# One block for the whole program, with one stage semaphore in place of the block ends of a graph network kernel

## The chip, the cores and the metric

The kernel runs on one core of one Trainium2 chip. The metric is the device time of one execution in microseconds (us); lower is better. The median of three executions is 4856.15 us.

## The reference

The input is a graph of 6250 nodes with 256 features and 100000 edges, sorted by destination. A layer norm and a ReLU are followed by three rounds of message passing with a maximum; the result is added to `x`; a second layer norm and ReLU are followed by one layer of graph attention with 8 heads, which is added too. Cut to what matters:

```python
def _pool_max(h, edge_src, edge_dst):
    pooled = jax.ops.segment_max(h[edge_src], edge_dst, num_segments=N)
    return jnp.where((cnt > 0)[:, None], pooled, 0)
...
h1 = relu(embeddings @ Wp1.T + bp1);  p1 = _pool_max(h1, edge_src, edge_dst)
x = relu(concatenate([embeddings, p1]) @ Wm1.T + bm1);  p2 = _pool_max(x, ...)
y2 = relu(concatenate([x, p2]) @ Wm2.T + bm2);  x = _layernorm(y2 + x, ln2_g, ln2_b);  p3 = _pool_max(x, ...)
y3 = relu(concatenate([x, p3]) @ Wm3.T + bm3);  x = _layernorm(y3 + x, ln3_g, ln3_b)
...
q, k, v = h @ Wq + bq, h @ Wk + bk, h @ Wv + bv          # q scaled, 8 heads
s = einsum('edh,edh->eh', q[rows], k[cols]);  m = segment_max(s, rows);  e = exp(s - m[rows])
out = segment_sum((e / segment_sum(e, rows)[rows])[:, None, :] * v[cols], rows)
return out.reshape(n, -1) @ Wo + bo
```

## The kernel before

Nodes lie in 49 tiles of 128 (`NT`), seven of them in a ring (`UN`). Edges lie by partition, 783 to each (`CH`). The program is a row of stages, and each stage is a `nc.Block()` of its own, in which each engine has one function with its instructions, written out without loops (`staged` writes them in a skewed order). Leaving a block puts the same things behind every engine's last instruction, at the line of the `with`: a branch, a DRAIN, and a meeting of all five engines through two semaphores, which GpSimd leads. The profile shows these with the line of the `with` statement.

The stages, with the line of their block and what ends them:

- `project` (block at L410): layer norm, first product, table `tab`. SyncE (SP) waits last for the stores of `tab`. Then `all_loaded` (L2200): a block in which only SP waits, for the first loads.
- `max_pass` (L526), three times: GpSimd gathers rows of `tab` for 783 edges of each partition, one indirect DMA of 128 rows each (L541); VectorE takes the running maximum (L561), ScalarE copies the state (L602, L604), SP stores three steps at a time to `hist` (L586) and waits in the end for the last of these stores (L590). Beside them fillers sort the edges (`Degrees`, `Sorting`, `Spread`); `Ahead` moves the attention weights on ScalarE in the third pass.
- `combine` (L1499), twice, and `combine_project` (L1647), once: carries across chains (L1411, L1415), 49 gathers of `hist` (L1438, L1669), the products. `combine_project` also writes `kvtab` and `xtab` from SP and scatters query rows to `qtab` from GpSimd (L1674), which waits in the end for those scatters (L1678).
- `attention_pass` (L1859): three gathers of `qtab` (L1863), then 78 batches of 12 gathers of `kvtab` by GpSimd (L1871), with six buffers.
- `carry_attention` (L2018): a chain through all engines that ends in GpSimd's scatters to `ahist` (L2108). `finish` (L2126): 49 gathers, last product, output.

Everything that one stage stores to HBM for the next is waited for by the engine that issued it, inside the stage. Sets of buffers are freed at the end of a stage and given to the next.

Of the kernel before, what the change touches and what calls it, by code (L numbers as in the profile page):

```python
# [22 lines left out]
P = 128  # L23
D = 256
# [78 lines left out]
def gnn_kernel(nc, x, src, dst, wp1, bp1, wm1, bm1, wm2, bm2, wm3, bm3, g2, b2, g3, b3,  # L103
# [40 lines left out]
    with ExitStack() as top:  # L144
# [68 lines left out]
        chain = Chain(nc.vector, sem("chain"))  # L213

        def block():
            return nc.Block()
# [188 lines left out]
        def project(weights, emit, stores, store_sp, per_out, now, later, beside=None, scatter=None, start=None):  # L405
# [4 lines left out]
            with scope() as st, block() as blk:  # L410
# [78 lines left out]
                if stores:  # L489
                    @blk.sync  # L490
                    def _(sp):
# [30 lines left out]
        def max_pass(G, side, tiles, marks=None, ahead=None):  # L522
            state = bank[3][:, 0:2 * D].rearrange("p (c f) -> p c f", c=2)
            state2 = bank[6][:, D:2 * D]

            with block() as blk:  # L526
                @blk.gpsimd
                def _(g):
                    if marks:
                        marks.pool(g)  # L530
                    side.start_pool(g)

                    def gather(i, b):
                        for k in range(J):
                            j, c = divmod(k, C)
                            r, at = b * STEPS + j, c * (CH // C) + (i * UB + b) * STEPS + j
                            if c == 0 and i:
                                g.wait_ge(s_kept[r].sem, s_kept[r].base + i * 16)
                            if i == 0 and r == RING - 1 and c == 0:
                                g.wait_ge(c_state.sem, c_state.base + 2)  # L540
                            g.indirect_dma_start(G[b][:, k, :], None, tab, bass.IndirectOffsetOnAxis(src_ix[:, at:at + 1], 0)).then_inc(s_in[r].sem, 16)  # L541
                    staged(g, NB, UB, [(0, gather), (0, side.pool(g))])

                @blk.vector
                def _(v):
                    if marks:
                        marks.vector(v)
                    side.start(v)
                    v.memset(G[UB - 1][:, J - C:J, :], 0.0).then_inc(c_fold.sem, 2)

                    def fold(k):
                        def stage(i, b):
                            j, c = divmod(k, C)
                            step = (i * UB + b) * STEPS + j
                            if c == 0:
                                arrived = s_in[b * STEPS + j]
                                v.wait_ge(arrived.sem, arrived.base + (i + 1) * (16 * C))
                            if c != 1:
                                v.wait_ge(c_state.sem, c_state.base + 2 * step + (2 if c else 1))
                            at = c * (CH // C) + step  # L560
                            ins = v.scalar_tensor_tensor(out=G[b][:, k, :], in0=state2 if c == 2 else state[:, c, :], scalar=reset[:, at:at + 1],  # L561
                                                         in1=G[b][:, k, :], op0=ALU.add, op1=ALU.max)
                            if c:
                                ins.then_inc(c_fold.sem, 1)
                        return stage

                    fillers, own = side.vector(v), {side.KEEP_AT: tiles.vector(v)}
                    stages = []
                    for k in range(J):
                        stages += [(0, fold(k))] + fillers.get(k, []) + own.get(k, [])  # L570
                    staged(v, NB, UB, stages)

                @blk.sync
                def _(sp):
                    if marks:
                        marks.sync(sp)
                    side.sync(sp)

                    def store(i, b):
                        for j in range(STEPS):  # L580
                            step = (i * UB + b) * STEPS + j
                            if step < NB * STEPS - 1:
                                sp.wait_ge(c_state.sem, c_state.base + 2 * (step + 2))
                            else:
                                sp.wait_ge(c_fold.sem, c_fold.base + 2 * (step + 2))
                            sp.dma_start(hist_p[:, step * C:(step + 1) * C, :], G[b][:, j * C:(j + 1) * C, :]).then_inc(s_kept[b * STEPS + j].sem, 16)  # L586
                    staged(sp, NB, UB, tiles.sync(sp) + [(0, store)] + (ahead.sync(sp) if ahead else []))
                    side.last_sync(sp)
                    for kept in s_kept:
                        sp.wait_ge(kept.sem, kept.base + (NB // UB) * 16)  # L590

                @blk.tensor
                def _(pe):
                    staged(pe, NB, UB, side.tensor(pe, *tiles.tensor(pe)))

                @blk.scalar
                def _(a):
                    def keep_state(step):
                        n, j = divmod(step, STEPS)
                        of = G[n % UB][:, j * C:(j + 1) * C, :]  # L600
                        a.wait_ge(c_fold.sem, c_fold.base + 2 * step + 3)
                        a.activation(state, of[:, 0:2, :], ACT.Copy).then_inc(c_state.sem, 1)  # L602
                        a.wait_ge(c_fold.sem, c_fold.base + 2 * step + 4)
                        a.activation(state2, of[:, 2, :], ACT.Copy).then_inc(c_state.sem, 1)  # L604

                    def keep_step(j):
                        def stage(i, b):
                            step = (i * UB + b) * STEPS + j
                            if step < NB * STEPS - 1:
                                keep_state(step)  # L610
                        return stage

                    fill, evac = tiles.scalar(a)
                    keep_state(-1)
                    staged(a, NB, UB, [(0, keep_step(0))] + side.scalar(a, evac) + fill + [(0, keep_step(j)) for j in range(1, STEPS)]
                           + (ahead.scalar(a) if ahead else []))
# [810 lines left out]
        def node_gathers(blk, pool, table, width, rows_of, carry=None, nodes=None):  # L1427
            @blk.gpsimd
            def _(g):
                if nodes:  # L1430
                    nodes.pool(g)
# [31 lines left out]
        class Ahead:  # L1463
# [6 lines left out]
            def __init__(self, sort, side):  # L1470
# [4 lines left out]
                self.arrived, self.keys_stored = sem("ahead_arrived"), side.stored  # L1475
# [4 lines left out]
            def sync(self, sp):  # L1480
# [4 lines left out]
                return [(self.LOADED, load, 1)]  # L1485

            def scalar(self, a):
                def move(to, given, scale):
                    def stage(i, b):
                        a.wait_ge(self.arrived, 16 * len(self.loads))  # L1490
                        a.activation(to.rearrange("p (h d) -> p h d", h=HEADS), given.rearrange("p (d h) -> p h d", h=HEADS), ACT.Copy, scale=scale)
# [3 lines left out]
        def combine(G, U, w, gain, bias, to_table, carry, beside=None):  # L1495
# [3 lines left out]
            with scope() as st, block() as blk:  # L1499
# [16 lines left out]
                def _(v):  # L1516
                    stats, recip, _ = norm_stages(v, None, lambda i, u: y[:, u, :])
# [34 lines left out]
                    if nodes:  # L1552
                        nodes.finish(v)

                @blk.scalar
                def _(a):
                    _, _, sqrt = norm_stages(None, a, None)
# [27 lines left out]
                def _(pe):  # L1585
                    carry.tensor(pe)
# [20 lines left out]
                if residual or to_table:  # L1607
                    @blk.sync
                    def _(sp):
                        def load(i, u):  # L1610
# [7 lines left out]
                        if to_table:  # L1618
                            for u in range(UN):
                                sp.wait_ge(s_st[u].sem, s_st[u].base + NT // UN * 16)  # L1620
            for c in (c_T, c_hT, c_mm, c_y, c_z):
# [13 lines left out]
        def combine_project(G, U, w, gain, carry, sort, beside):  # L1635
# [11 lines left out]
            with scope() as st, block() as blk:  # L1647
# [15 lines left out]
                def _(g):  # L1663
                    carry.pool(g)
# [16 lines left out]
                def _(v):  # L1681
                    stats, recip, _ = norm_stages(v, None, lambda i, u: y[:, u, :])
# [39 lines left out]
                    def emit(i, u):  # L1722
# [3 lines left out]
                        if i:  # L1726
# [5 lines left out]
                                       (NT + 12, lambda i, u: beside(v), 1)])  # L1732

                @blk.scalar
                def _(a):
                    _, _, sqrt = norm_stages(None, a, None)
# [32 lines left out]
                def _(pe):  # L1769
                    carry.tensor(pe)  # L1770
# [38 lines left out]
                def _(sp):  # L1809
# [503 lines left out]
```

## Time and profile before

| what | us |
|---|---|
| median of 3 executions (4855.05 to 4858.15) | 4856.15 |
| the profiled execution, device time | 4848.88 |
| its span, first to last instruction | 4847.1 |
| `project` and `all_loaded` | 79.35 |
| the three `max_pass` | 989.13, 985.07, 997.90 |
| the two `combine` | 86.08, 104.19 |
| `combine_project` | 253.98 |
| `attention_pass` | 1243.00 |
| `carry_attention`, `finish` | 29.36, 79.07 |

The stage times are the lengths of the windows between one release of all engines and the next, read from the trace; their sum is the span. A name with a q behind it (SPq, POOLq) is the engine's sequencer, which works ahead of the engine; waits, branches, DRAINs and semaphores run there and count in no busy time. PE is TensorE, DVE VectorE, ACT ScalarE, POOL GpSimd.

### The profile page before, as it was taken

To read this page: it belongs to the slowest core of one execution; us is meant where nothing else is said; L and a number is where in the kernel's file an instruction comes from. 1 tells how busy PE (TensorE), PEld (TensorE's weight loads), DVE (VectorE), ACT (ScalarE), POOL (GpSimd) and SP (SyncE) were. 2 spreads that over 40 slices of the span, in tenths; PEclk is the share of its full clock that TensorE was granted. 3 is DMA by queue.
4 is the path that set the end of the run, shared out by engine and by line. 5 is a ranking of instruction groups with operands and counts; after the bars stand their busy time and mean duration, and the time that the engine had idled before them with its cause. 6 is when DMAs were issued, how large, how long until landed. Compare 5 with 4: busy or idle time off the path is not lost. (4 is left out here: it accounts for less than half of the span.)

```text
span 4847.1 us, 27940 instructions
## 1 busy us (share of the span) xinstructions
PE 1710.1 (35%) x5261; PEld 1035.5 (21%) x5261; DVE 3135.9 (65%) x6298; ACT 1096.5 (23%) x2585; POOL 3461.3 (71%) x3612
## 2 busy tenths in 40 slices
PE   5434322106233312025222200019644454445546
PEld 4222211005111100014111100006322222222224
DVE  7888887645444444437455533338488888888886
ACT  5333322223222222224222222225200000000001
POOL 4777777766777777766777777765377777777764
PEclk8555555558555555557555555559867777777778
DMA  5666666656777777756666766655478887887875
GB/s 193 217 209 210 211 210 209 212 181 209 255 257 255 259 248 242 242 189 209 223 212 221 233 212 209 211 185 192 143 239 256 253 254 255 257 255 255 253 227 178
DMA packets 451437, 1083.65 MB, mean 224 GB/s; under 512 B 82637, under 2 KB 178524, under 8 KB 451263
## 3 DMA queue, kind: packets, MB, share of 16 engines
q0 software_dynamic: 203376, 598.29, 42.7%
q1 hardware_dynamic: 247886, 483.58, 26.9%
q14 instruction: 131, 1.07, 0.1%
q8 instruction: 44, 0.72, 0.1%
HBM read 656.78 MB, written 425.20 MB: 223 GB/s over the span
## 5 line engine op out<-in xcount | busy, mean ns | idle before, releaser
L541 POOL DMA_INDIRECT G<-tab,pass_lists x2349 | 2228.3, 949 | 725.0 <-issue 714.8
L561 DVE SCALAR_TENSOR_TENSOR G<-tail,pass_lists,G 128x256 f32<-128x256 f32 x1566 | 699.1, 479 | 1304.5 <-DMA G<-tab,pass_lists 1296.3
L1871 POOL DMA_INDIRECT kv<-kvtab,dst_ix x936 | 923.5, 987 | 285.1 <-issue 285.1
L602 ACT ACTIVATE tail<-G 128x512 f32<-128x512 f32 x783 | 471.0, 602 | 1768.1 <-DVE G L561 1726.3
L678 PE MATMUL tail<-weights,hT 128*128 128x256 f32 x588 | 304.9, 674 | 551.7 <-ACT hT L655 551.7
L1977 PE MATMUL tail<-kv,ident 128*128 128x512 f32 (+1 forms) x624 | 301.7, 653 | 360.9 <-DVE kv L1909 360.9
L1977 PE MATMUL trio<-kv,ident 128*128 128x512 f32 (+1 forms) x624 | 294.4, 640 | 295.4 <-DVE kv L1909 295.4
L604 ACT ACTIVATE wide<-G 128x256 f32<-128x256 f32 x783 | 296.8, 379 | 382.4 <-DVE G L561 371.1
L561 DVE SCALAR_TENSOR_TENSOR G<-wide,pass_lists,G 128x256 f32<-128x256 f32 x783 | 372.5, 476 | 0.8
L1903 DVE TENSOR_TENSOR kv<-kv,wide 128x3072 f32<-128x3072 f32 x78 | 261.7, 3355 | 167.9 <-DMA kv<-kvtab,dst_ix 167.9
L672 PE MATMUL tail<-ident,h 128*128 128x128 f32 x294 | 95.1, 426 | 625.5 <-DVE U L641 582.3
L678 PEld LDWEIGHTS tail<-weights,hT 128*128 128x128 f32 x588 | 172.6, 324 | 634.6 <-ACT hT L655 608.1
L1985 ACT ACTIVATE wide<-weights 128x120 f32<-128x120 f32 x78 | 21.4, 274 | 1205.9 <-DVE weights L1960 1205.9
L1977 PEld LDWEIGHTS tail<-kv,ident 128*128 128x128 f32 x624 | 157.6, 260 | 505.4 <-DVE kv L1909 377.0
L1909 DVE TENSOR_TENSOR kv<-kv,wide 128x3072 f32<-128x3072 f32 x78 | 261.1, 3347 | 0.3 <-ACT wide L1985 0.3
L1913 DVE TENSOR_REDUCE s<-kv 128x96 f32<-128x3072 f32 x78 | 261.0, 3346 | 0.0
L1379 PE MATMUL trio<-ident,G 128*128 128x128 f32 x18 | 4.5, 424 | 697.0 <-PEq L526 697.0
L1977 PEld LDWEIGHTS trio<-kv,ident 128*128 128x128 f32 x624 | 154.4, 255 | 435.4 <-DVE kv L1909 311.1
L1104 PE MATMUL trio<-hot 128*128 128x196 bf16 x783 | 142.2, 369 | 195.7 <-DVE hot L955 195.7
L672 PEld LDWEIGHTS tail<-ident,h 128*128 128x128 f32 x294 | 42.0, 201 | 734.3 <-issue 689.7
L955 DVE TENSOR_TENSOR hot<-wide,key_high 128x2156 bf16<-128x2156 f32 x72 | 170.4, 2367 | 0.0
L1104 PEld LDWEIGHTS trio<-hot 128*128 128x128 bf16 x783 | 114.1, 148 | 218.7 <-DVE hot L955 207.7
(340 smaller groups left out, 3281.4 us busy)
## 6 DMA issues: line engine op xcount, KB each, us to landing
hist<-G SPq DMA_DIRECT2D x783, 384.0 KB, 3.0
G<-tab,pass_lists POOLq DMA_INDIRECT x2349, 3.2
ahist<-state SPq DMA_DIRECT2D x78, 408.0 KB, 3.4
qtab<-zeros SPq DMA_DIRECT2D x78, 384.0 KB, 4.3
weights<-qtab SPq DMA_DIRECT2D x59, 384.0 KB, 5.7
tab<-o SPq DMA_DIRECT2D x147, 128.0 KB
kv<-kvtab,dst_ix POOLq DMA_INDIRECT x936, 3.9
h<-tab SPq DMA_DIRECT2D x98, 128.0 KB, 3.9
```

Of the source, the lines that this page charges most:

```text
L541: g.indirect_dma_start(G[b][:, k, :], None, tab, bass.IndirectOffsetOnAxis(src_ix[:, at:at + 1], 0)).then_inc(s_in[r].sem, 16)
L561: ins = v.scalar_tensor_tensor(out=G[b][:, k, :], in0=state2 if c == 2 else state[:, c, :], scalar=reset[:, at:at + 1], in1=G[b][:, k, :], ...
L602: a.activation(state, of[:, 0:2, :], ACT.Copy).then_inc(c_state.sem, 1)
L604: a.activation(state2, of[:, 2, :], ACT.Copy).then_inc(c_state.sem, 1)
L678: m = pe.matmul(self.product, self.hT[:, k * P:(k + 1) * P], self.w[:, k, :], start=(k == 0), stop=(k == KC - 1))
L955: v.tensor_tensor(to[n % self.RING][:, 0:some, :, :].rearrange("p k l e -> p (k l) e"), self.iota[:, None, 0:width].to_broadcast([P, 2 * s ...
L1104: m = pe.matmul(self.sums, self.low[n % self.RING][:, k, :, :], self.high[n % self.RING][:, k, :, :], start=(n == 0 and k == 0), stop=(n = ...
L1871: g.indirect_dma_start(kvs[n % KB][:, k, :], None, kvtab, bass.IndirectOffsetOnAxis(dst_ix[:, at:at + 1], 0)).then_inc(s_kv[n % KB], 16)
L1903: v.tensor_tensor(keys, keys, query[:, None, :, :].to_broadcast([P, SLOT, R, D]), ALU.mult).then_inc(c_scored, 1)
L1909: v.tensor_tensor(vals, vals, by_slot[:, :, None, :].to_broadcast([P, GATHERS, HD, HEADS]), ALU.mult).then_inc(c_weighed, 1)
L1913: keep("sums", i * UB + b, v.tensor_reduce(scores().rearrange("p e r h -> p (e r) h"), kvs[(i * UB + b) % KB][:, :, 0:D].rearrange("p k (h ...
L1977: m = pe.matmul(sums[n % 2][:, rs, :], ident[:, :], kvs[n % KB][:, e * R + rs.start:e * R + rs.stop, D:KV], start=(e == 0), stop=(e == SLO ...
```

## The change

One `nc.Block()` is opened at the start and closed at the end of the program, and all stages add their functions to it, so an engine's instructions follow each other with no branch, DRAIN or meeting between stages. In their place stands one semaphore, `s_stage`. Every engine function of every stage begins with a wait for its present base value, and the engines whose work the next stage needs raise it by one at the end of their part. SP raises it in every stage. VectorE raises it in `max_pass`, in the first `combine` and in `combine_project`; GpSimd in `combine_project` and `carry_attention`. TensorE and ScalarE never do. `all_loaded` is gone: its two waits stand at the end of SP's part of `project`. VectorE gets a one-element `memset` with a wait for it at the end of `max_pass`, and `Ahead` counts ScalarE's moves in a semaphore, for which SP waits after its last store of the third pass. Whole functions are only indented less. `finish` has no `s_stage` increment: the block ends behind it.

```diff
-        def block():
-            return nc.Block()
+        s_stage = Count(sem("s_stage"))
+
+        whole = ExitStack()
+        blk = whole.enter_context(nc.Block())
...
-            with scope() as st, block() as blk:
+            with scope() as st:
...
+                        if start:
+                            sp.wait_ge(s_load, load_base[0])
+                            sp.wait_ge(s_lists, (6 + 13) * 16)
+                        sp.sem_inc(s_stage.sem, 1)
+            s_stage.close(1)
...
+            @blk.gpsimd
+            def _(g):
+                g.wait_ge(s_stage.sem, s_stage.base)
...
+                staged(v, NB, UB, stages)
+                chain.link(v.memset(stat[:, 0, 0:1], 0.0))
+                v.sem_inc(s_stage.sem, 1)
...
+                for kept in s_kept:
+                    sp.wait_ge(kept.sem, kept.base + (NB // UB) * 16)
+                sp.sem_inc(s_stage.sem, 1)
...
+            s_stage.close(2)
...
-                return [(self.LOADED, load, 1)]
+
+                def await_moves(i, b):
+                    sp.wait_ge(self.moved, len(self.moves))
+                return [(self.LOADED, load, 1), (NB - 1, await_moves, 1)]
...
-                        a.activation(to.rearrange(...), given.rearrange(...), ACT.Copy, scale=scale)
+                        a.activation(to.rearrange(...), given.rearrange(...), ACT.Copy, scale=scale).then_inc(self.moved, 1)
...
                     if nodes:
                         nodes.finish(v)
+                        v.sem_inc(s_stage.sem, 1)
...
                     for u in range(UN):
                         g.wait_ge(s_put[u], (NT // UN) * 16)
+                    g.sem_inc(s_stage.sem, 1)
...
                     g.wait_ge(s_misc.sem, m0 + 32 * R)
+                    g.sem_inc(s_stage.sem, 1)
...
-            all_loaded()
...
             finish(w_o, v_o)
+            whole.close()
```

## Rows read from the trace of the kernel before

**Rows 1.** The page's first lines: span, busy us, share of the span, count
```profile
span 4847.1 us, 27940 instructions
PE 1710.1 (35%) x5261; PEld 1035.5 (21%) x5261; DVE 3135.9 (65%) x6298; ACT 1096.5 (23%) x2585; POOL 3461.3 (71%) x3612
```

**Rows 2.** Windows, second `max_pass` and attention: length, busy us (PE, PEld, DVE, ACT, POOL)
```profile
1154.56:2139.63 985.07, 211.87 (x394) 102.52 (x394) 448.42 (x1059) 262.04 (x571) 740.24 (x783) 0.54 0.76 246
...
3495.70:4738.70 1243.00, 596.07 (x1248) 312.02 (x1248) 1061.01 (x1016) 22.66 (x79) 926.38 (x939) 0.71 0.79 249
```

**Rows 3.** The page's costliest groups, GpSimd's gathers: busy, mean ns, idle before them
```profile
L541 POOL DMA_INDIRECT G<-tab,pass_lists x2349 | 2228.3, 949 | 725.0 <-issue 714.8
...
L1871 POOL DMA_INDIRECT kv<-kvtab,dst_ix x936 | 923.5, 987 | 285.1 <-issue 285.1
```

**Rows 4.** Line L526, first `max_pass` end: ns min/median/max, first and last start
```profile
L526 POOLq DRAIN  x1: 20206/20206/20206, 1047.1 to 1047.1; - x1
...
L526 DVEq DRAIN  x1: 1298/1298/1298, 1064.2 to 1064.2; - x1
L526 SPq COMPARE_BRANCH  x1: 33/33/33, 1068.1 to 1068.1; - x1
...
L526 SPq EVENT_SEMAPHORE  x1: 17/17/17, 1068.5 to 1068.5; - x1
```

**Rows 5.** Line L410, the block of `project`
```profile
L410 POOLq EVENT_SEMAPHORE  x2: 17/17/17, 78.4 to 78.5; - x2
...
L410 SPq COMPARE_BRANCH  x1: 38/38/38, 78.3 to 78.3; - x1
...
L410 ACTq EVENT_SEMAPHORE  x1: 17/17/17, 78.6 to 78.6; - x1
```

**Rows 6.** Line L2200, the block of `all_loaded`
```profile
L2200 SPq EVENT_SEMAPHORE  x1: 17/17/17, 79.3 to 79.3; - x1
```

**Rows 7.** Line L526, third `max_pass` end
```profile
L526 POOLq DRAIN  x1: 21652/21652/21652, 3219.9 to 3219.9; - x1
...
L526 SPq COMPARE_BRANCH  x1: 33/33/33, 3240.9 to 3240.9; - x1
...
L526 SPq EVENT_SEMAPHORE  x1: 17/17/17, 3241.7 to 3241.7; - x1
```

**Rows 8.** Line L1647, the end of `combine_project`
```profile
L1647 SPq COMPARE_BRANCH  x1: 33/33/33, 3485.8 to 3485.8; - x1
...
L1647 POOLq COMPARE_BRANCH  x1: 41/41/41, 3486.8 to 3486.8; - x1
L1647 POOLq DRAIN  x1: 8537/8537/8537, 3487.0 to 3487.0; - x1
L1647 SPq EVENT_SEMAPHORE  x1: 17/17/17, 3495.7 to 3495.7; - x1
```

**Rows 9.** Timeline of GpSimd, 3478 to 3502: start, us, what, idle before
```profile
3484.37 0.98 POOL L1674 DMA_INDIRECT qtab<-G,first_ix  x1 [3.04 <-DVE G L1729]
3496.44 0.98 POOL L1863 DMA_INDIRECT pass_lists<-qtab,chain_ix  x1 [11.09 <-POOLq L1647]
```

**Rows 10.** Window inside the DRAIN at L1647; the last columns are clock, DMA, GB/s
```profile
3487.00:3495.50 8.50, 0.00 (x0) 0.00 (x0) 0.00 (x0) 0.00 (x0) 0.00 (x0) 0.50 0.00 0
```

**Rows 11.** Timeline of GpSimd inside `combine_project`: scatter and gather in turn
```profile
3291.21 1.13 POOL L1674 DMA_INDIRECT qtab<-G,first_ix  x1 [10.51 <-DVE G L1729]
3292.65 0.97 POOL L1669 DMA_INDIRECT pool<-hist,node_ix  x1 [0.30 <-issue]
```

**Rows 12.** Line L2018, the end of `carry_attention`
```profile
L2018 POOLq COMPARE_BRANCH  x1: 38/38/38, 4767.2 to 4767.2; - x1
L2018 POOLq DRAIN  x1: 534/534/534, 4767.3 to 4767.3; - x1
L2018 SPq EVENT_SEMAPHORE  x1: 17/17/17, 4768.0 to 4768.0; - x1
```

**Rows 13.** Timeline of VectorE behind the first `max_pass`: a small MEMSET
```profile
1069.46 0.06 DVE L1392 MEMSET G<- 128x2 f32 x1
```

More of the change, by code:

```diff
@@ L524, in max_pass @@
             state2 = bank[6][:, D:2 * D]
[L526 to L568, printed above, removed]
-                    for k in range(J):
[L570 to L616, printed above, removed]
@@ new lines, in _, with fold, stage @@
+            @blk.vector
+            def _(v):
+                v.wait_ge(s_stage.sem, s_stage.base)
+                if marks:
+                    marks.vector(v)
+                side.start(v)
+                v.memset(G[UB - 1][:, J - C:J, :], 0.0).then_inc(c_fold.sem, 2)
+                def fold(k):
+                    def stage(i, b):
+                        j, c = divmod(k, C)
+                        step = (i * UB + b) * STEPS + j
+                        if c == 0:
+                            arrived = s_in[b * STEPS + j]
+                            v.wait_ge(arrived.sem, arrived.base + (i + 1) * (16 * C))
+                        if c != 1:
+                            v.wait_ge(c_state.sem, c_state.base + 2 * step + (2 if c else 1))
+                        at = c * (CH // C) + step
+                        ins = v.scalar_tensor_tensor(out=G[b][:, k, :], in0=state2 if c == 2 else state[:, c, :], scalar=reset[:, at:at + 1],
+                                                     in1=G[b][:, k, :], op0=ALU.add, op1=ALU.max)
+                        if c:
+                            ins.then_inc(c_fold.sem, 1)
+                    return stage
+                fillers, own = side.vector(v), {side.KEEP_AT: tiles.vector(v)}
+                stages = []
+                for k in range(J):
+                    stages += [(0, fold(k))] + fillers.get(k, []) + own.get(k, [])
+                staged(v, NB, UB, stages)
+                chain.link(v.memset(stat[:, 0, 0:1], 0.0))
+                v.sem_inc(s_stage.sem, 1)
@@ new lines, in _, with keep_state, keep_step, stage @@
+            @blk.tensor
+            def _(pe):
+                pe.wait_ge(s_stage.sem, s_stage.base)
+                staged(pe, NB, UB, side.tensor(pe, *tiles.tensor(pe)))
+            @blk.scalar
+            def _(a):
+                a.wait_ge(s_stage.sem, s_stage.base)
+                def keep_state(step):
+                    n, j = divmod(step, STEPS)
+                    of = G[n % UB][:, j * C:(j + 1) * C, :]
+                    a.wait_ge(c_fold.sem, c_fold.base + 2 * step + 3)
+                    a.activation(state, of[:, 0:2, :], ACT.Copy).then_inc(c_state.sem, 1)
+                    a.wait_ge(c_fold.sem, c_fold.base + 2 * step + 4)
+                    a.activation(state2, of[:, 2, :], ACT.Copy).then_inc(c_state.sem, 1)
+                def keep_step(j):
+                    def stage(i, b):
+                        step = (i * UB + b) * STEPS + j
+                        if step < NB * STEPS - 1:
+                            keep_state(step)
+                    return stage
+                fill, evac = tiles.scalar(a)
+                keep_state(-1)
+                staged(a, NB, UB, [(0, keep_step(0))] + side.scalar(a, evac) + fill + [(0, keep_step(j)) for j in range(1, STEPS)]
+                       + (ahead.scalar(a) if ahead else []))
@@ new lines, in _, with gather @@
+            @blk.gpsimd
+            def _(g):
+                g.wait_ge(s_stage.sem, s_stage.base)
+                for r in range(R):
+                    g.indirect_dma_start(begun[:, r, :], None, qtab, bass.IndirectOffsetOnAxis(chain_ix[:, r:r + 1], 0)).then_inc(s_begun, 16)
+                def gather(i, b):
+                    n = i * UB + b
+                    if n >= KB:
+                        g.wait_ge(c_taken.sem, c_taken.base + n - KB + 1)
+                    for k in range(R * SLOT):
+                        at = (k % R * NBA + n) * SLOT + k // R
+                        g.indirect_dma_start(kvs[n % KB][:, k, :], None, kvtab, bass.IndirectOffsetOnAxis(dst_ix[:, at:at + 1], 0)).then_inc(s_kv[n % KB], 16)
+                staged(g, NBA, UB, [(0, gather)])
@@ new lines, in _, with add_slots @@
+            @blk.tensor
+            def _(pe):
+                pe.wait_ge(s_stage.sem, s_stage.base)
+                def add_slots(i, b):
+                    n = i * UB + b
+                    pe.wait_ge(c_weighed, n + 1)
+                    if n >= 2:
+                        pe.wait_ge(c_batch.sem, c_batch.base + n - 1)
+                    for e in range(SLOT):
+                        for rs in BANKS:
+                            m = pe.matmul(sums[n % 2][:, rs, :], ident[:, :], kvs[n % KB][:, e * R + rs.start:e * R + rs.stop, D:KV], start=(e == 0), stop=(e == SLOT - 1))
+                    m.then_inc(c_taken.sem, 1)
+                staged(pe, NBA, UB, [(0, add_slots)])
@@ L2004, in attention_pass @@
+            s_stage.close(1)
             c_taken.close(NBA)
@@ L2017, in carry_attention @@
             ALL = P * R
-            with ExitStack() as st, block() as blk:
+            with ExitStack() as st:
                 wide_z = sb(st, "wide_z", [P, 2, R, G8, HEADS])
@@ L2125, in finish @@
         def finish(w, bias):
-            with ExitStack() as st, block() as blk:
+            with ExitStack() as st:
                 rz = sb(st, "rz", [P, UN, HEADS])
```

289 lines of the change are left out of this document (158 added, 131 removed).

## The prediction, made before the changed kernel ran

> **What bounds the kernel now.** I read four views, in this order: the page, the windows of each stage, the sequencer rows at the line of each block, and the timeline of GpSimd around the one stage end that stood out.
>
> The page gives the span, 4847.1 us, and the busy shares. GpSimd is the busiest engine at 71% [rows 1]. The windows say more than the share. In the second `max_pass`, 985.07 us long, GpSimd is busy for 740.24 us in 783 gathers, and each takes 1.26 us of the stage (985.07 / 783). In attention 936 gathers (of the 939) fill almost all of 1243 us [rows 2]. The idle time in front of both kinds of gather is put down to "issue" nearly to the last microsecond: 285.1 of 285.1 us in attention, 714.8 of 725.0 in the passes [rows 3]. So in the four long stages GpSimd waits for nobody once it has begun. The stage is its start plus a fixed row of gathers plus a tail. A stage that starts earlier ends earlier by the same amount, and that holds along the whole chain of stages, since none may start before its predecessor is done, before and after the change. So what a boundary gives back arrives whole at the end, and I only have to find what each boundary costs between the last thing that really had to be waited for and the first instruction behind it.
>
> The rows at a block's line show this. At the end of the first `max_pass` the last wait of SP is passed at its branch, at 1068.1 us. The release of SP, the last step of the meeting, is at 1068.5 [rows 4]. This is 0.3 to 0.4 us, with rows rounded to a tenth. SP was the last to come: VectorE's DRAIN began at 1064.2 and took 1.3 us, GpSimd's began at 1047.1 and took 20.2, so it was over at 1067.3, less than a microsecond ahead of SP [rows 4]. So a long DRAIN of GpSimd is normally hidden behind the last stores. The question at each boundary is whether it is hidden there too.
>
> **The change, part by part.**
>
> *Ordinary boundaries.* The same pair of rows, from SP's branch to SP's release, stands 0.3 us apart at five of the boundaries: behind the first and second `max_pass`, both `combine`, and attention. The row of the first of these five is shown [rows 4]. The new form is one increment of a semaphore and one wait of each engine. For it I have a row: at `project`'s end GpSimd's second semaphore instruction starts at 78.5 and ScalarE's release at 78.6 [rows 5], so one hop costs about 0.1 us by the rounded rows; I can't see it being less than 0.05 or more than 0.1. I take 0.25 us saved at each of five, together **1.25 us** (bounds 1.0 to 1.5).
>
> *`project` and `all_loaded`.* Here two meetings follow each other: SP's branch at 78.3 [rows 5], last release at 79.3 [rows 6], 1.0 us. In their place come SP's two waits, for loads that have long landed, and one hop. **0.85 us** saved (0.7 to 0.9).
>
> *Third `max_pass`.* SP reaches its branch at 3240.9, but GpSimd's DRAIN started at 3219.9 and took 21.652 us, so it ended at 3241.55 and everyone left at 3241.7 [rows 7]. GpSimd raises nothing in this stage after the change. From 0.8 us, less one hop: **0.7 us** (0.6 to 0.75).
>
> *`combine_project`.* This is the large one. SP is done at 3485.8. GpSimd passes its last wait, for the scatters to `qtab`, at 3486.8 and then sits in a DRAIN for 8.537 us, so that all engines leave at 3495.7 [rows 8]. In these 8.5 us no engine computes and the DMA engines move 0 GB/s [rows 10]: nothing of the program is being done. After the change GpSimd raises `s_stage` behind the same wait, at 3486.8. The distance to the release is 8.9 us, less one hop: **8.8 us**. What attention does after its release is the same as before; its first gather started 0.74 us after the release (3496.44 less 3495.7 [rows 8, 9]) and should start that long after the new one, near 3487.6.
>
> Is the DRAIN a delay of itself, or work of GpSimd that must be done before the next gather in any case? The trace before has a nearer case than the boundary: within `combine_project` a scatter of the same kind ends at 3292.34 and the next gather starts at 3292.65, 0.30 us later [rows 11]; and within the passes thousands of gathers follow at this distance [rows 3]. Before a DRAIN, GpSimd takes the next indirect DMA at once, so I take the DRAIN as avoidable. The bounds are 8.8 us, all of it, and 0.3 us, if its 8.5 us come back in front of the next gather.
>
> The Trainium skill knows the instruction. "VectorE: DVE Perf Modes", section "The DRAIN you can't avoid", tells of DRAINs that are boilerplate on all five engines and take about 12 ns, constant. By that price the DRAINs at the block ends would be worth nothing, and the estimate by it for this boundary would be an ordinary 0.25 us and for the whole change 3.8 us. This trace disagrees for GpSimd: its rows have 20.2, 21.7 and 8.5 us [rows 4, 7, 8].
>
> *`carry_attention`.* GpSimd is last here: branch at 4767.2, DRAIN of 0.534 us, SP's release at 4768.0 [rows 12]. 0.8 less one hop: **0.75 us** (0.6 to 0.75).
>
> *The end of the program.* The one block still ends with a meeting, as before. Nothing.
>
> *What is added.* The `memset` of one element and its wait on VectorE at the end of `max_pass`: a MEMSET of two elements took 0.06 us [rows 13]. VectorE starts its DRAIN at 1064.2 and ends it, with its last work, at 1065.5; SP comes at 1068.1 [rows 4]. The addition has 2.6 us of cover, the landing of the last `hist` store; if that were gone it would cost 0.1 to 0.2 us in each of three passes. SP's wait for ScalarE's moves stands behind the last store of the third pass, and only SP's waits for the landings stand behind it; the moves are scheduled some 20 batches earlier (the last at turn 65 of 87). Nothing. The waits at the head of the engine functions stand where the meeting stood; behind each are all the instructions of that engine for the stage, which was so before. No DMA, no gather and no computation is moved to another engine or queue, and none crosses a boundary, since SP's stores are still awaited before SP raises.
>
> *Sum.* 1.25 + 0.85 + 0.7 + 8.8 + 0.75 = 12.35 us. Against its own trace: the profiled execution took 4848.88 us, 1.8 more than its span, so it would come to 4836.5. The median of the runs is 7.3 us above that execution, a difference of 0.15% that I leave as it is. From the median: 4856.15 - 12.35 = **4843.8 us**. Its own range is 4841.5 to 4846: the boundaries at their bounds give 11.7 to 12.7, and the rest is how well two builds repeat; the three runs shown spread over 3.1 us.
>
> **Rivals.**
>
> *The DRAIN's work comes back.* If GpSimd must finish some bookkeeping of its indirect DMAs before it can take the first one of attention, the 8.5 us stay, and perhaps the 0.5 us in the third pass too. For it: the DRAIN outlasts the landing of the scatter, which GpSimd had already waited for [rows 8], so something is going on in the engine, and the DRAIN behind the similar scatters of `carry_attention` takes only 0.534 [rows 12], so it is not a fixed price. Against it: rows 11. Then 12.35 - 8.5 - 0.5 = 3.35 us are saved: 4852.8.
>
> *Slower: gathers become dearer.* GpSimd's gathers are 3285 in number, with a mean of 949 and 987 ns [rows 3]. The second mean is above the first by 38 ns, or 36 us over 936 gathers, so something in attention slows some of them. If the new start (other engines at another phase, TensorE and ScalarE entering with no DRAIN behind them, GpSimd with its bookkeeping undone) made this worse, it would be paid 3285 times. From 3.8 ns on the mean (12.35 / 3285) it eats the whole gain; at 10 ns the kernel is 20 us slower, near 4876. Against it: every engine is released at the same moment in either form, and order and waits inside a stage are unchanged, so the phase has no reason to move.
>
> *The change doesn't do what it says*, for example since leaving and entering were cheaper than the rows let it seem, and a wait on a raised semaphore costs as much as the meeting. Then only the DRAIN goes, some 8.5 + 0.5 us: 4847.2. This is within 0.2%, just.
>
> *More is given back:* the engines' ends are no longer flushed, and something shorter appears at each start. I have no row that prices it; by the rows 4 the most that one boundary holds beyond the forecast is 0.1 us. I keep a small chance for a gain beyond 16 us from what I don't see.
>
> **How the numbers follow.** The bound below which a measurement of this kernel can't tell a change from none is about 0.2%, 9.7 us: 4846.4 to 4865.9. The forecast, with a gain over 9.7, has a chance of 0.67; the DRAIN that comes back 0.18; gathers dearer 0.06, of which 0.05 end slower by over 0.2% and 0.01 eat only the gain; the cheap meeting 0.05; more given back 0.04. Faster: 0.67 + 0.04 = 0.71. Same: 0.18 + 0.05 + 0.01 = 0.24. Slower: 0.05. The range for 8 in 10 takes in the forecast, the cheap meeting and the returning DRAIN: 4841 to 4854.
>
> **What would show it.** In the profile of the changed kernel no DRAIN or branch stands at the stage lines; the first gather of attention starts about 2.5 us after the last scatter's end, not 11.09 us [rows 9]; each stage is as long as before to within a microsecond or two, except that the third pass, `combine_project` and `carry_attention` end 0.7, 8.8 and 0.75 us sooner. If the first gather of attention starts early but itself takes 9 us, or the gathers behind it do, the first rival holds. If the means of L541 and L1871 move by more than 3 ns, the second does. I would be wrong by more than a little if GpSimd without any DRAIN ran its gathers differently; this trace has no stage of that sort.

## The result, and the profile after

The changed kernel takes 4840.85 us in the median of 10 executions (4833.64 to 4844.78), the kernel before 4853.01 us in 10 (4849.45 to 4858.15). The ratio is 0.9973, with a 95% interval of 0.9965 to 0.9981. So the change saves 12.2 us by the medians (4853.01 - 4840.85), where the prediction had 12.35; by the interval it is 9.2 to 17.0 us. The time forecast, 4843.8, was set from a median of 4856.15 over three runs; over ten the median of before is 3.1 us lower, and the measured 4840.85 lies 0.15 us below the low end of the range.

The page of the changed kernel, its first lines and the two groups that answer to [rows 1, 3]:

```profile
span 4831.8 us, 27852 instructions
PE 1708.9 (35%) x5261; PEld 1034.7 (21%) x5261; DVE 3137.1 (65%) x6301; ACT 1096.1 (23%) x2585; POOL 3452.3 (71%) x3612
...
L547 POOL DMA_INDIRECT G<-tab,pass_lists x2349 | 2227.7, 948 | 725.6 <-issue 714.3
...
L1905 POOL DMA_INDIRECT kv<-kvtab,dst_ix x936 | 922.7, 986 | 285.1 <-issue 285.1
```

The work is the same: VectorE has three MEMSETs more, and a gather takes what it took, to 1 ns in the mean. The lines are renumbered; L547 was L541, L1905 was L1871, L1700 was L1674. Below are windows of three stages of the changed kernel, from one increment of the last engine to the next; the first and the third answer to [rows 2]. The first window begins 0.7 us too early: SyncE's increment stands at 1154.4, so the second `max_pass` is 984.6 us long (1154.4 to 2139.0), where it was 985.07.

```profile
1153.70:2139.10 985.40, 210.54 (x394) 101.54 (x394) 448.35 (x1060) 262.05 (x571) 740.46 (x783) 0.54 0.75 246
3238.90:3484.70 245.80, 206.44 (x796) 133.54 (x796) 173.13 (x692) 99.61 (x294) 107.92 (x104) 0.95 0.48 161
3484.70:4725.40 1240.70, 597.24 (x1248) 312.83 (x1248) 1061.09 (x1016) 22.66 (x79) 925.61 (x939) 0.71 0.79 249
```

The second is `combine_project`: 245.8 us where it took 253.98. GpSimd's timeline at its end, in the changed kernel, shows why, and answers to [rows 9]:

```profile
3482.19 0.98 POOL L1700 DMA_INDIRECT qtab<-G,first_ix  x1 [3.03 <-DVE G L1757]
3485.63 0.98 POOL L1897 DMA_INDIRECT pass_lists<-qtab,chain_ix  x1 [2.45 <-POOLq L1705]
```

The idle time between the last scatter and attention's first gather (the hole, below) is 2.45 us in place of 11.09. What released the gather is line 1705, GpSimd's own increment. This row answers to the branch, DRAIN and release of [rows 8]:

```profile
L1705 POOLq EVENT_SEMAPHORE  x1: 43/43/43, 3484.6 to 3484.6; - x1
```

At the other end of the scale is an ordinary boundary, the end of `max_pass` in the changed kernel. The rows show SyncE's increment and who waited for it, and answer to [rows 4]:

```profile
L601 SPq EVENT_SEMAPHORE  x3: 28/28/28, 1067.7 to 3238.9; - x3
...
  POOL G L1338: 5.9, 1
```

With VectorE's own increment ahead of it, one instruction of 28 ns does what took a branch, five DRAINs and the meeting.

### The profile page after: what moved, and what is told of

Same layout as the page of the kernel before. It is cut to its first block, busy times and chain, and to the rows that moved or that the text cites. A ratio compares the mean times of both kernels' runs of the same rounds, so it can differ in the third digit from the quotient of the medians.

```text
span 4831.8 us, 27852 instructions
## 1 busy us (share of the span) xinstructions
PE 1708.9 (35%) x5261; PEld 1034.7 (21%) x5261; DVE 3137.1 (65%) x6301; ACT 1096.1 (23%) x2585; POOL 3452.3 (71%) x3612
## 4 chain that ended last, share of the span: by engine, by line
POOL 66%; issue 22%; PE 7%; DVE 3%; DMA 2%; ACT 0%; POOLq 0%; DVEq 0%; SPq 0%; ACTq 0%
POOL G L547 46%; POOL kv L1905 19%; PE tail L1835 2%; PE wide L1835 1%; PE wide L1624 1%; DMA tab<-o 1%; DMA pool<-ahist,node_ix 0%; PE wide L467 0%; POOL pool L1453 0%; PE trio L1816 0%; PE tail L1816 0%; DVE o L1561 0%; DVE stat L387 0%; PE tail L1624 0%; DVE G L1546 0%
## 5 line engine op out<-in xcount | busy, mean ns | idle before, releaser
L547 POOL DMA_INDIRECT G<-tab,pass_lists x2349 | 2227.7, 948 | 725.6 <-issue 714.3
L1905 POOL DMA_INDIRECT kv<-kvtab,dst_ix x936 | 922.7, 986 | 285.1 <-issue 285.1
```

Source lines behind the costliest of these rows:

```text
L1905: g.indirect_dma_start(kvs[n % KB][:, k, :], None, kvtab, bass.IndirectOffsetOnAxis(dst_ix[:, at:at + 1], 0)).then_inc(s_kv[n % KB], 16)
```

## The experiments

The runs fell on four chips. The first group (`drain_back`, `only_this`, `all_but_this`, `raise_then_drain`) ran where the kernel before takes 5447.44 us (35 runs), the second (`meet20`, `hops20`, `intervals`, `late_double`) where it takes 5460.88 us (19), the third (`early_drain`, `counts`, `only_this_again`) where it takes 4844.25 us (21), and `after_again` where it takes 4844.65 us (12). Times are compared only with the kernel before on the same chip. The ratios and their intervals are those on record; they can differ a little from the quotient of the two medians.

On the two slower chips the times scatter over 12 to 42 us, and another engine sets the pace. This is the chain that ended last, as shares of the span, in the changed kernel's own trace and then in `drain_back`'s:

```profile
POOL 66%; issue 22%; PE 7%; DVE 3%; DMA 2%; ACT 0%; POOLq 0%; DVEq 0%; SPq 0%; ACTq 0%
```

```profile
DVE 36%; issue 23%; another core or an unknown queue 22%; PE 8%; POOL 4%; ACT 4%; DMA 2%; POOLq 0%; DVEq 0%; SPq 0%; ACTq 0%
```

The prediction's premise, that GpSimd waits for nobody once it has begun, doesn't hold on that chip, so a few microseconds need not arrive whole at its end. For the slower chips the rows decide.

**The DRAIN put back alone.**

```diff
                     for u in range(UN):
                         g.wait_ge(s_put[u], (NT // UN) * 16)
+                    g.drain()
                     g.sem_inc(s_stage.sem, 1)
```

> The changed kernel with one DRAIN of GpSimd put back at the end of combine_project, behind its last wait and ahead of its increment of the stage semaphore. Theory (the DRAIN is where the gain lies): the DRAIN takes about 8.5 us again, the first gather of attention starts 8.6 us later than in the changed kernel, and the median comes to 3.6 us below before, about 4849.4. Rival (the gain is spread over the stages, because no engine is drained between them): the DRAIN costs little at this one place and the median stays within 3 us of the changed kernel's 4840.9.

Measured: 5440.76 us, 0.9992 of before (0.9974 to 1.0009). The time alone separates nothing. The rows of this run do. They are the DRAIN at its line, and GpSimd's timeline around it.

```profile
L1705 POOLq DRAIN  x1: 9292/9292/9292, 3954.0 to 3954.0; - x1
```

```profile
3951.59 0.98 POOL L1700 DMA_INDIRECT qtab<-G,first_ix  x1 [3.03 <-DVE G L1758]
3964.10 0.98 POOL L1898 DMA_INDIRECT pass_lists<-qtab,chain_ix  x1 [11.53 <-POOLq L1705]
```

One instruction brings back the hole of 11 us. It is 9.3 us long here, 0.8 more than the one it stands for [rows 8]. In `counts`, further down, the same DRAIN stands in a run on a faster chip, where it takes 9.292 us too and the hole is 11.53 us.

**Only this boundary changed, and all but this one.** Both are made from the changed kernel with a function that closes the block and opens a new one. `only_this` calls it at every stage end but that between `combine_project` and attention, `all_but_this` at that one alone.

```diff
         blk = whole.enter_context(nc.Block())
+
+        def join():
+            nonlocal blk
+            whole.close()
+            blk = whole.enter_context(nc.Block())
...
                 combine_project(G, U, w_m3b, v_g3, Carry(G, blocked, 0), sort, find_empty)
+                join()
```

> The changed kernel, but with the block closed and opened again at every stage end except that between combine_project and attention; the two blocks of project and all_loaded stay one. Theory: this one boundary gives 8.8 us and the missing all_loaded 0.7, so the median lies 9.5 us below before, about 4843.5. Rival (gain spread over all stages): a tenth to a third of the gain, 1 to 4 us, about 4850.

> The complement: stage semaphore everywhere, but the block closed and opened between combine_project and attention. Theory: 12.35 less 8.8, so 3.5 us below before, about 4849.5, with a DRAIN of 8.5 us in the trace at that place. Rival (gain spread): 8 to 11 us below before, about 4843.

Measured: `only_this` 5432.71 us, 0.998 of before (0.9962 to 0.9998); `all_but_this` 5435.48 us, 0.999 (0.9976 to 1.0004). By the medians the second lies 12.0 us below before, where the theory had 3.5 and the rival 8 to 11. Its time is a miss for the theory, though its interval reaches from 13 us below before to 2 above and so refutes neither. The timeline of `only_this`, and then that of `all_but_this`:

```profile
3952.32 0.98 POOL L1705 DMA_INDIRECT qtab<-G,first_ix  x1 [3.04 <-DVE G L1762]
3955.57 0.98 POOL L1902 DMA_INDIRECT pass_lists<-qtab,chain_ix  x1 [2.27 <-POOLq L1710]
```

```profile
3936.23 0.98 POOL L1705 DMA_INDIRECT qtab<-G,first_ix  x1 [3.03 <-DVE G L1762]
3948.99 0.98 POOL L1902 DMA_INDIRECT pass_lists<-qtab,chain_ix  x1 [11.78 <-POOLq L221]
```

The hole follows the block end at this one place (L221 is where the block is closed). The first of the two was run again on a faster chip:

> The kernel with blocks everywhere but between combine_project and attention, once more, to narrow its interval. Theory: 9.5 us below before in the median; combine_project ends at the landing of the last scatter, with the first gather of attention 2.3 us behind the scatter's end. Rival (gain spread over all stages): 1 to 4 us below before.

Measured: 4835.14 us against 4844.25, a ratio of 0.9982 (0.9973 to 0.9991), 9.1 us by the medians. That fits the 9.5 of the theory; the rival's 1 to 4 us lie just outside the interval, whose upper end is a saving of 4.4 us (0.0009 of 4844).

**The DRAIN behind the increment.** All other engines leave, GpSimd alone drains.

```diff
                     g.sem_inc(s_stage.sem, 1)
+                    g.drain()
```

> The changed kernel with the DRAIN behind GpSimd's increment: all other engines are released at once, only GpSimd drains. Theory (GpSimd paces attention, so its own lateness counts whole): as much lost as with the DRAIN ahead of the increment, first gather 8.5 us late, median about 4849.4. Rival (what costs is that all engines are held): VectorE, SyncE and TensorE start on time and take up the delay, median within 3 us of 4840.9.

Measured: 5440.55 us, 0.9993 (0.9979 to 1.0006), which doesn't separate the two. In attention the gathers of `kvtab` have 401.6 us of idle time ahead of them on that chip (in `drain_back`) in place of 285.1, so the question whether GpSimd's lateness counts whole stays open in time. The timeline shows that the lateness itself is the same, 11.60 us, now put down to "issue" since no other engine or semaphore is to blame:

```profile
3956.12 0.98 POOL L1700 DMA_INDIRECT qtab<-G,first_ix  x1 [3.03 <-DVE G L1758]
3968.70 0.98 POOL L1898 DMA_INDIRECT pass_lists<-qtab,chain_ix  x1 [11.60 <-issue]
```

**The price of a block end by itself,** and of the handover that replaces it.

```diff
+                for _ in range(20):
+                    with block() as extra:
+                        @extra.sync
+                        def _(sp):
+                            sp.wait_ge(s_load, load_base[0])
```

> The kernel before with 20 more blocks behind the first combine, each with only a wait of SyncE for loads that landed long ago. It prices a block end by itself. Theory: by the two releases around all_loaded a whole extra block takes 0.7 to 0.8 us, so 20 add 15 us and each shows DRAINs of GpSimd of some 0.05 us, since none of its DMAs is outstanding. Rival (the meeting is almost free, what costs is the DRAIN behind real DMAs): under 0.3 us each, 6 us in all.

Measured: 5466.17 us, 1.0006 of before (0.9993 to 1.002), so 15 us more is outside the interval (10.9 at most). The rows of the extra blocks' line:

```profile
L2269 POOLq DRAIN  x20: 34/34/102, 1363.9 to 1372.0; - x20
L2269 SPq COMPARE_BRANCH  x20: 33/33/33, 1364.0 to 1372.1; - x20
...
L2269 SPq EVENT_SEMAPHORE  x20: 17/17/17, 1364.3 to 1372.4; - x20
```

From the first to the twentieth release it is 8.1 us, so a whole empty block costs 0.43 us (8.1 / 19), between my 0.7 and the rival's 0.3. SyncE's branch and its release are 0.3 us apart, as at the ordinary boundaries. GpSimd's DRAIN, with nothing issued since the last, takes 34 ns.

```diff
+                @blk.sync
+                def _(sp):
+                    sp.wait_ge(s_stage.sem, s_stage.base)
+                    for n in range(20):
+                        sp.sem_inc(ping, 1)
+                        sp.wait_ge(pong, n + 1)
+                    sp.sem_inc(s_stage.sem, 1)
...
+                    for n in range(20):
+                        v.wait_ge(ping, n + 1)
+                        v.sem_inc(pong, 1)
```

> The changed kernel with a stage put behind the first combine in which SyncE and VectorE pass a semaphore to and fro 20 times, 40 hops, and one more hop of the stage semaphore. Theory: a hop is 0.05 to 0.1 us, so 2 to 4 us more. Rival (a handover by semaphore costs as much as the meeting it replaces, 0.3 us): 12 us more.

Measured: 5450.01 us, 0.998 of before (0.9966 to 0.9994). The changed kernel alone didn't run on this chip. Against before, the theory would have 8 to 10 us less and the rival about none; the medians have 10.9 less, and the interval excludes a saving of nothing. SyncE's 20 increments, at their line:

```profile
L2317 SPq EVENT_SEMAPHORE  x20: 17/17/17, 1374.0 to 1376.0; - x20
```

19 round trips in 2.0 us are 38 hops of 0.053 us. The handover costs a fifth of the meeting.

**What sets the length of the DRAIN.** A first look put DRAINs into attention behind a growing number of gathers.

```diff
+                    if n in (0, 1, 3, 7, 15, 31, 63):
+                        g.drain()
```

> The changed kernel with a DRAIN of GpSimd in attention after batches 0, 1, 3, 7, 15, 31 and 63, so behind 12 to 384 gathers since the last one (15 behind the start of the stage). Theory A (the DRAIN waits for the outstanding gathers and a fixed clean-up): each ends 5 to 8 us after the last gather has been issued, whatever their number, some 50 us more in all. Theory B (it pays for bookkeeping of every DMA since the last DRAIN): the length grows with the number, and the one behind 384 gathers is several times the one behind 12.

Measured: 5460.67 us, one execution. GpSimd still had gathers to run when these DRAINs came, so their rows mix two things: 21.1 us for the first and 21.9 for the last hold those gathers too. Counted from the end of the last gather they run for 9.3, 3.1, 3.4, 4.9, 7.9, 5.9 and 6.9 us. That is neither constant (A) nor growing to the end (B).

Does it wear off if one waits? Twelve large MEMSETs on VectorE hold GpSimd up, and then it drains twice:

```diff
+                    g.wait_ge(late, 1)
+                    g.drain()
+                    g.drain()
                     g.sem_inc(s_stage.sem, 1)
...
+                    for _ in range(12):
+                        chain.link(v.memset(y, 0.0))
+                    v.sem_inc(late, 1)
```

> The changed kernel; at the end of combine_project GpSimd waits, behind its scatters' landing, another 12 us or more for VectorE (12 large MEMSETs), then drains twice. Theory A (the clean-up runs by itself once the DMAs have landed): the first DRAIN is short, under 1 us. Theory B (the clean-up is done only when it is asked for): the first DRAIN again takes about 8.5 us. In both the second takes under 0.2 us.

Measured: 5472.13 us, one execution. Both DRAINs:

```profile
L1708 POOLq DRAIN  x1: 9292/9292/9292, 3978.6 to 3978.6; - x1
```

```profile
L1709 POOLq DRAIN  x1: 40/40/40, 3987.9 to 3987.9; - x1
```

The last scatter had ended at 3956.4, 22 us earlier, and the DRAIN still takes 9.292 us, to the nanosecond what it took without the pause. So nothing was cleared while GpSimd idled here; the time is spent when the DRAIN comes, and the second DRAIN takes 40 ns.

Then the numbers alone, with every gather landed before each DRAIN:

```diff
+                g.wait_ge(s_begun, 16 * R)
+                g.drain()
...
+                    if n in (0, 2, 5, 10, 18, 34):
+                        g.wait_ge(s_kv[n % KB], (n // KB + 1) * (16 * GATHERS))
+                        g.drain()
```

> The changed kernel with a DRAIN at the end of combine_project and then, in attention, behind 3, 12, 24, 36, 60, 96 and 192 gathers, each time only when GpSimd has waited until the last of them has landed. It measures the DRAIN alone. Theory (0.05 us and 0.082 us a DMA, ceiling near 9.3): 9.3, then 0.3, 1.0, 2.0, 3.0, 5.0, 7.9 and 9.3 us. Rival (the length in the middle of attention came from gathers still in flight, not from their number): all of them under 1 us, or all about the same.

Measured: 4885.42 us, one execution. The DRAINs of its two lines in attention, behind 3, 12, 24, 36, 60, 96 and 192 gathers:

```profile
L1900 POOLq DRAIN  x1: 288/288/288, 3503.7 to 3503.7; - x1
```

```profile
L1911 POOLq DRAIN  x1: 1017/1017/1017, 3522.2 to 3522.2; - x1
L1911 POOLq DRAIN  x1: 1997/1997/1997, 3556.3 to 3556.3; - x1
L1911 POOLq DRAIN  x1: 2977/2977/2977, 3607.6 to 3607.6; - x1
L1911 POOLq DRAIN  x1: 4937/4937/4937, 3690.4 to 3690.4; - x1
L1911 POOLq DRAIN  x1: 7877/7877/7877, 3821.9 to 3821.9; - x1
L1911 POOLq DRAIN  x1: 5917/5917/5917, 4079.7 to 4079.7; - x1
```

Six of them lie on one line to within 6 ns: (7877 - 288) / (96 - 3) = 81.6 ns for each DMA, and some 43 ns besides. The number of DMAs that a DRAIN is charged for by this line is called its debt below. [Rows 8, 12] lie on the line too: 104 DMAs make 8.53 us (8.537 there), 6 make 0.533 (0.534). The seventh does not. 192 gathers cost 5.917 us, what 72 would, that is 192 less 120. The ceiling that I had expected isn't one: the debt falls back somewhere on the way. Two other rows fall short in a like way. In `intervals` the DRAIN behind 384 gathers runs 6.91 us from the end of the last one, what 84 would cost, that is 384 less 300. In the kernel before, the DRAIN behind the 783 gathers of the first `max_pass` [rows 4] ends 5.2 us after the last of them, what 63 would cost, that is 783 less 720. All three shortfalls are multiples of 60. But the 9.292 us that a DRAIN took when none had come since the start would be 113 DMAs of 2567, which isn't short by such a multiple, so a step of 60 is a guess. Where the debt falls back, and at whose cost, the runs don't show; no gather in attention is longer than 2 us.

**The DRAIN earlier, the blocks kept.** If the price goes by the number, it can be paid where GpSimd idles. In the kernel before:

```diff
                         g.indirect_dma_start(qtab, bass.IndirectOffsetOnAxis(first_ix[:, t:t + 1], 0), qo[:, u, :], None,
                                              bounds_check=NOROW - 1, oob_is_err=False).then_inc(s_put[u], 16)
+                        if t == 31:
+                            g.drain()
```

> The kernel before, blocks and all, with one line more: GpSimd drains behind the scatter of tile 31 in combine_project, where it has 3 us of idle time between scatters. The runs so far fit a DRAIN that takes 0.05 us and 0.082 us for each indirect DMA since the last one (104 of them: 8.54; 6: 0.534), with a ceiling near 9.3. Theory (it is a price for each DMA, paid when the DRAIN comes): the early one takes 87 DMAs, 7.1 us and the landing, hidden in GpSimd's idle time; the one at the block end has 17 left and takes 1.4 us, so combine_project becomes 7.1 us shorter, and the kernel 7 us faster with its blocks kept. Rival (the DRAIN behind scatters to qtab takes its 8.5 us whatever came before): no change, 8.5 us again.

Measured: 4837.80 us against 4844.25, a ratio of 0.9986 (0.9977 to 0.9995), 6.5 us by the medians, where 7 were expected. `combine_project` took 248.1 us (release to release, 3240.7 to 3488.8), 5.9 less than before. The early DRAIN and the one at the block end:

```profile
L1677 POOLq DRAIN  x1: 8514/8514/8514, 3415.9 to 3415.9; - x1
```

```profile
L1647 POOLq DRAIN  x1: 1432/1432/1432, 3487.2 to 3487.2; - x1
```

17 DMAs cost 1.432 us (by the line, 1.43). The early row holds the scatter of tile 31 as well, which ended at 3417.30; from there the DRAIN runs for 7.1 us, and the line has 7.14 for 87 DMAs. GpSimd's timeline behind it shows how the delay is taken up, the next scatters following at 0.30 and 0.41 us where 3 us of idle time used to be:

```profile
3425.24 1.29 POOL L1674 DMA_INDIRECT qtab<-G,first_ix  x1 [7.95 <-issue]
3426.84 0.98 POOL L1674 DMA_INDIRECT qtab<-G,first_ix  x1 [0.30 <-issue]
3428.23 1.13 POOL L1674 DMA_INDIRECT qtab<-G,first_ix  x1 [0.41 <-issue]
```

So one line in the old kernel has about half of the gain of the whole change.

**The changed kernel once more.**

> The changed kernel itself once more, on another day's chip, to see what of the miss was level and what was gain. Theory (the sum of 12.35 us was right and the median of before moved under it): 12.35 us below whatever before takes here, a ratio of 0.9975 at 4850 us, though before itself may lie 10 us off 4856.15. Rival (the profiled executions, 15.3 us apart, show the true gain): 15 us or more, a ratio of 0.9969 or less.

Measured: 4831.51 us (8 runs) against 4844.65 (12 runs), a ratio of 0.9973 (0.9962 to 0.9983), 13.1 us by the medians. The theory had 12.35 and the rival 15 or more, a ratio of 0.9969 or less; the medians side with the theory, while the interval holds both. It is the lowest median of all versions run.

## Why the gain was forecast right and the time missed

**The range missed by its level.** The step that failed is the term from which the gain was taken, "From the median: 4856.15 - 12.35", with "the three runs shown spread over 3.1 us" as the measure of "how well two builds repeat". Ten runs of the same kernel before have a median of 4853.01, 3.1 us lower, and in two later series it was 4844.25 and 4844.65. The prediction had a warning: it saw the profiled execution 7.3 us below the median of three and left that difference as it was. Taken from 4853.01, the forecast gain gives 4840.66, against 4840.85 measured. The miss of the range by 0.15 us and the near agreement of the gain are both finer than the measurement, whose interval is 9.2 to 17.0 us; it confirms the large term, not the small ones.

**The boundary of `combine_project`: right.** 8.8 us were forecast. The hole went from 11.09 to 2.45 us, 8.64; the first gather began 1.0 us after GpSimd's increment (3485.63 less 3484.6), where 0.74 was taken. The whole stage is 8.2 us shorter in this trace (245.8 for 253.98). That GpSimd's DRAIN is the cause is shown in the rows by putting it back, and in the time by `only_this_again`, which keeps 9.1 us of the gain, and by `early_drain`, which shortens the DRAIN, keeps the blocks and gains 6.5 us.

**The ordinary boundaries: right in size.** The meeting measures 0.3 us from SyncE's branch to the release, a hop 0.053, so each should give back 0.25. No single one can be read from the stage lengths: the first `combine` is 0.6 us longer in the changed trace (86.7, 1067.7 to 1154.4), the second `max_pass` 0.5 shorter. `project` ends at 78.4 where the second release stood at 79.35, 0.9 us for a forecast 0.85, and `carry_attention` takes 28.4 us for 29.36, 1.0 for 0.75. The sum of all terms but `combine_project`, 3.55 us, was not measured by itself: the median of `all_but_this` lies 12 us below before with an interval that holds zero. `only_this_again` keeps the 0.7 us of `all_loaded`, so the full change should save 2.85 us more than it; the two differ by 4.0 us (13.1 less 9.1, on two chips), within the error of either.

**Third pass and `carry_attention`.** Only these two and `combine_project` had a DRAIN of GpSimd that came last [rows 7, 8, 12]. In the changed trace the third pass is 3.0 us shorter (994.9 from 2244.0 to 3238.9, where it took 997.90) for a forecast 0.7, attention 2.3 us shorter for 0.25, while the second `combine` is 0.8 us longer (105.0). The two profiled executions lie 15.3 us apart in all, 3 more than the medians. These surpluses need not be the change: in `early_drain`, where both stages are the old code, attention took 1237.8 us (release to release, 3488.8 to 4726.6) against 1243.00, and the third pass 995.6 (2245.1 to 3240.7) against 997.90. A long stage of the same code differs by 2 to 5 us between two traces.

**The rivals.** The returning DRAIN is refuted: without one, the gathers of attention start early, at 2.45 us of idle time, and take what they took. In `late_double` the debt stayed through 22 us of rest. That fits the guess behind the rival, of work not yet done, though what this work is no row shows; what was wrong in it is that the next gather must wait for it. Dearer gathers: the means went from 949 to 948 and from 987 to 986 ns. The cheap meeting: it is 0.3 us, not nothing.

**The Trainium skill.** The 12 ns that the Trainium skill gives in "VectorE: DVE Perf Modes", section "The DRAIN you can't avoid", are for the boilerplate DRAINs ahead of and behind a kernel. The prediction held them against DRAINs at block ends, of which that passage doesn't speak. The empty blocks of `meet20` are near it on ScalarE and VectorE, with 8 and 10 ns, but not on GpSimd, with 34. With GpSimd's DMAs landed behind it, the same instruction took up to 9.3 us. The prediction's 3.8 us for the whole change by that price is also too high: the third pass and `carry_attention` would have been ordinary boundaries too, which makes 2.85 (1.25 + 0.85 + 3 times 0.25).

## What to carry to other kernels

Ask at each block end who comes last, and look at the sequencer rows of GpSimd: here its DRAIN cost 82 ns for each DMA that it issued since the last DRAIN, up to 104 of them, and 5.2 to 9.3 us behind more. Idle time ahead of it didn't lessen it. Where stores hide it, leave it; where GpSimd itself ends the stage, hand over by a semaphore behind its own landing wait, or drain earlier, where it idles. The meeting of all engines is worth 0.25 us, so ten of them are not what one rewrites a program for. And when a gain of 0.25% is forecast, state it as a difference: the level of the same kernel moved by 0.17% between two series of runs (4853.01 to 4844.65), and by 3.1 us between the first three runs and all ten of one.

## What the hardware showed that was not expected

A DRAIN of GpSimd 22 us after its last DMA had ended takes as long as one right behind it, 9.292 us. Its length rises by 81.6 ns a DMA up to 96 (and 104, before the change) and is shorter again at 192, 5.917 us. And the same program runs at 4844 us on one chip and 5447 us on another, with nearly the same mean granted clock in the profiled executions (0.615 and 0.605). There the mean gather of `tab` takes 951 ns, 2 more than before the change [rows 3], but GpSimd is idle for 1121.7 us before these gathers instead of 725.0, as this row of `drain_back` shows, and the row of that line behind it tells most of the difference.

```profile
L547 POOL DMA_INDIRECT G<-tab,pass_lists x2349 | 2234.8, 951 | 1121.7 <-issue 735.5
```

```profile
  DMA hist<-G: 373.5, 104
```

In 104 places GpSimd waits there for a store to `hist` to land before it may use the buffer again, 373.5 us in all; the same view of the kernel before has no such wait. Why these stores take longer on that chip is open.
